# Per-token steps of a state-space block moved into the patch embedding's chunk pipeline

## The reference

```python
u = up_x @ W_up + b_up                      # up_x: the normed tokens
left, right = jnp.split(u, 2, axis=-1)      # 128 features each
conv = sum(conv_w[:, k] * xp[:, k:k + Lq, :] for k in range(3)) + conv_b
x = silu(conv)
delta = softplus(x @ W_delta + b_delta)
Bm = x @ W_B + b_B ; Cm = x @ W_C + b_C
# then over 37 positions: h = exp(delta*A)*h + (delta*x)*Bm ; y_t = h . Cm
gated = (y + D_skip * x) * silu(right)
```

## Time and profile before

| what | value |
|---|---|
| device time, median of 3 runs | 1154.97 us (1151.09 to 1156.85) |
| device time of the profiled execution | 1155.57 us |
| its span in the trace | 1153.4 us |
| busy: PE, DVE, ACT, POOL | 935.1, 657.2, 508.3, 305.0 us |
| DMA | 96.06 MB, 92705 packets |
| TensorE's granted clock over the run, in tenths, 40 slices | `9999656898898998998989999999979999998579999` |

### The profile page before, as it was taken

How to read it: one execution, slowest core, us unless ns; L and a number is a source line. 1 busy time by engine, 2 the same in 40 slices (tenths; PEclk the granted TensorE clock), 3 DMA queues, 4 the chain that set the end, 5 groups by cost and what they waited for, 6 DMA issues and landing times.

```text
span 1153.4 us, 17650 instructions
## 1 busy us (share of the span) xinstructions
PE 935.1 (81%) x5925; PEld 597.4 (52%) x5926; DVE 657.2 (57%) x1129; ACT 508.3 (44%) x1028; POOL 305.0 (26%) x361
## 2 busy tenths in 40 slices
PE   8996272677777777669999999989999997559996
PEld 6763230233333233235677777757767664336564
DVE  2534833588888889865454444437777673313332
ACT  1227371777777887424322222234444532223332
POOL 5913911133333430000000000035444430422222
PEclk9999656898898998989999999979999998579999
DMA  6292369422222211434521111000000000522230
GB/s 234 92 344 94 96 198 237 95 51 51 50 52 50 53 32 34 175 149 199 180 70 58 42 42 42 0 1 1 1 1 0 0 2 1 222 100 83 78 94 25
DMA packets 92705, 96.06 MB, mean 83 GB/s; under 512 B 64350, under 2 KB 78687, under 8 KB 90976
## 3 DMA queue, kind: packets, MB, share of 16 engines
q1 hardware_dynamic: 89904, 87.91, 25.1%
q0 software_dynamic: 2736, 7.30, 1.7%
HBM read 61.57 MB, written 34.59 MB: 83 GB/s over the span
## 4 chain that ended last, share of the span: by engine, by line
PE 64%; ACT 12%; DVE 9%; issue 6%; SPq 4%; DMA 4%; another core or an unknown queue 0%; POOL 0%; ACTq 0%; DVEq 0%; POOLq 0%
PE ps L526 8%; PE ps L585 8%; PE ps L1142 6%; ACT mem L1572 5%; PE ps L1024 4%; PE ps L1428 4%; PE ps L1444 4%; PE ps L1339 3%; PE ps L1273 3%; PE ps L395 3%; PE ps L1102 3%; PE ps L403 3%; SPq L783 2%; ACT mem L1597 2%; PE ps L1285 2%
## 5 line engine op out<-in xcount | busy, mean ns | idle before, releaser
L981 POOL TENSOR_TENSOR mem<-mem,sm 128x296 f32<-128x296 f32 x128 | 87.0, 713 | 364.3 <-ACT mem L1662 321.5
L1572 ACT ACTIVATE mem<-ps 128x512 f32<-128x512 f32 x288 | 154.0, 637 | 42.9 <-DMA factor_rows<-mem 30.3
L959 POOL TENSOR_SCALAR mem<-mem,sm 128x16 f32<-128x16 f32 x148 | 102.7, 716 | 203.5 <-PE ps L1142 203.5
L1102 PE MATMUL ps<-mem 64*128 64x128 bf16 x1140 | 92.0, 230 | 53.6 <-ACT mem L1572 44.3
L1102 PEld LDWEIGHTS ps<-mem 64*128 64x128 bf16 x1140 | 56.0, 99 | 121.6 <-ACT mem L1572 102.4
L1883 DVE TENSOR_TENSOR ps<-mem 128x512 f32<-128x512 f32 x144 | 93.5, 694 | 42.1 <-ACT mem L1597 41.6
L526 PE MATMUL ps<-mem 128*128 (+1 forms) x384 | 108.6, 413 | 0.6 <-DVE mem L499 0.6
L1597 ACT ACTIVATE mem<-ps 128x512 f32<-128x512 f32 x148 | 82.4, 609 | 54.0 <-PE ps L1109 53.8
L1142 PE MATMUL ps<-mem 128*32 128x512 f32 x592 | 87.3, 663 | 22.1 <-issue 13.6
L1109 PE MATMUL ps<-mem 64*128 64x512 bf16 x296 | 76.7, 421 | 31.5 <-DVE ps L1883 21.6
L1875 DVE TENSOR_TENSOR mem<-mem 128x1024 f32<-128x1024 f32 x72 | 87.7, 1218 | 25.0 <-ACT mem L1572 25.0
(11 more groups left out here) (224 smaller groups left out, 1613.0 us busy)
## 6 DMA issues: line engine op xcount, KB each, us to landing
mem<-gates SPq DMA_DIRECT2D x7, 1184.0 KB, 6.1
mem<-in_w SPq DMA_DIRECT2D x2, 4096.0 KB, 17.5
slots<-mem SPq DMA_DIRECT2D x1, 6682.0 KB, 23.8
mem<-slots SPq DMA_DIRECT2D x26, 257.0 KB, 2.7
mem<-in_patches SPq DMA_DIRECT2D x7, 864.0 KB, 4.8
mem<-factor_rows SPq DMA_DIRECT2D x296, 16.0 KB, 1.8
mem<-factor_rows SPq DMA_DIRECT2D x37, 128.0 KB, 2.3
mem<-delta_rows SPq DMA_DIRECT2D x9, 512.0 KB, 4.5
```

The costliest lines, as they stand in the source:

```text
L959: nc.gpsimd.tensor_scalar(c_win4[:, t % SLOTS * 2 + r, :, w0:w0 + 8].rearrange("p j (x i) -> p j x i", i=2)[:, :, :, i], c_all[:, r * 16:r ...
L1102: mm = nc.tensor.matmul(ps[:, ring_bank(at_), e * BT:(e + 1) * BT], a_stat[64 * r:64 * r + 64, g, e, :], delta_in[b % 2][64 * r:64 * r + 6 ...
L1572: nc.scalar.activation(decay_slots[b % 2][:, :, 4 * k:4 * k + 4], ps[:, ring_bank(at_), :].rearrange("p (e t) -> p t e", e=4), ACT.Exp).th ...
```

## The change

The step functions get five more stages. The hardware loop is replaced by 15 written-out steps, `chunks_in_step` with `LAG = 7`. In step k: the SiLU argument of chunk k-2; SiLU of chunk k-3 as exp(min(a,0) - log(1 + exp(-|a|))) for x and gate together (592 columns: two exponentials and a logarithm on ACT, two instructions on DVE); the products with that and C and delta's argument for chunk k-4; softplus and dx for chunk k-5; delta's pieces for chunks k-6 and k-7. No table load is left but the first. The products use the banks of the mean (4) and of the variance (5), so mean and variance wait for their evictions.

```diff
+LAG = 7
+def chunks_in_step(step):
+    for k in range(NCH + LAG):
+        step(k, k % 2, lambda d: 0 <= k - d < NCH)
...
             pe.wait_ge(embedded, k * 2 + 4)
+            if on(5):
+                pe.wait_ge(z_copied, k - 4)
             pe_mean(pe, ln, k - 1, 4)
         if on(0):
             products(1).then_inc(embedded_ps, 1)
+        if on(4):
+            c = k - 4
+            i = pair_rows(c)[0]
+            pe.wait_ge(x_ready, c + 1)
+            pe.wait_ge(LN["logvar"], LN_FROM[ln] + min(k - 2, NCH - 1) + 3)
+            if c >= 1:
+                pe.wait_ge(c_copied, c)
+            nc.tensor.matmul(ps[64 * i:64 * i + 64, 5, 0:CH], w_c, paired(xs, c * IC, IC),
+                             start=True, stop=True)
+            pe.wait_ge(LN["centered"], LN_FROM[ln] + min(k - 1, NCH - 1) + 3)
+            if c >= 1:
+                pe.wait_ge(z_copied, c)
+            nc.tensor.matmul(ps[:, 4, 0:CH], W("w_delta"), paired(xs, c * IC, IC),
+                             start=True, stop=True).then_inc(zc_ps, 1)
...
             mm.then_inc(up_ps, 1)
         if on(1):
+            if on(4):
+                pe.wait_ge(c_copied, k - 3)
             pe_var(pe, ln, k - 1, 1 - j, 5)
-    staged(pe, pe_embed, 2)
+    w_b, w_c = W("w_bc")[:, 0:N], W("w_bc")[:, N:2 * N]
+    chunks_in_step(pe_embed)
...
     def act_embed(k, j, on):
+        if on(3):
+            c = k - 3
+            now = sig[:, :, c % 2, :]
+            act.wait_ge(sig_cut, 2 * c + 1)
+            nc.scalar.activation(now, now, ACT.Exp).then_inc(sig_step, 1)
+            act.wait_ge(sig_step, 3 * c + 1)
+            nc.scalar.activation(now, now, ACT.Ln, bias=1.0).then_inc(sig_step, 1)
         if on(1):
             act_square(act, ln, k - 1, 1 - j)
...
+        if on(5):
+            c = k - 5
+            cs = ds(c * CH, CH)
+            act.wait_ge(soft_abs, c + 1)
+            nc.scalar.activation(delta[:, cs], delta[:, cs], ACT.Exp).then_inc(soft_step, 1)
+            act.wait_ge(soft_step, 2 * c + 1)
+            nc.scalar.activation(delta[:, cs], delta[:, cs], ACT.Ln, bias=1.0).then_inc(soft_step, 1)
+        if on(7):
+            c = k - 7
+            i, qs = pair_rows(c)
+            act.wait_ge(piece_cut, 2 * c + 1)
+            nc.scalar.activation(delta_part[:, 1, i, :, qs], cut_now, ACT.Copy).then_inc(piece_copied, 1)
+        if on(6):
+            c = k - 6
+            i, qs = pair_rows(c)
+            act.wait_ge(delta_ready, c + 1)
+            nc.scalar.activation(delta_part[:, 0, i, :, qs],
+                                 delta[:, c * CH:(c + 1) * CH].rearrange("p (q l) -> p l q", q=IC),
+                                 ACT.Copy).then_inc(piece_copied, 1)
+        if on(4):
+            c = k - 4
+            i, qs = pair_rows(c)
+            half = slice(64 * i, 64 * i + 64)
+            act.wait_ge(zc_ps, c + 1)
+            nc.scalar.activation(c_all[half, qs, :], ps[half, 5, 0:CH].rearrange("p (q l) -> p q l", q=IC),
+                                 ACT.Identity, bias=S("b_cc")[half]).then_inc(c_copied, 1)
+            if c >= 2:
+                act.wait_ge(delta_ready, c - 1)
+            nc.scalar.activation(z_now[:, c % 2, :], ps[:, 4, 0:CH], ACT.Identity,
+                                 bias=S("b_delta")).then_inc(z_copied, 1)
         if on(1):
             act_rstd(act, ln, k - 1, 1 - j, 5)
...
+        if on(3):
+            c = k - 3
+            cs = slice(c * CH, (c + 1) * CH)
+            now = sig[:, :, c % 2, :]
+            act.wait_ge(sig_cut, 2 * c + 2)
+            nc.scalar.activation(now, now, ACT.Exp).then_inc(sig_step, 1)
+    chunks_in_step(act_embed)
...
     def dve_embed(k, j, on):
+        if on(4):
+            c = k - 4
+            dve.wait_ge(sig_step, 3 * c + 3)
+            nc.vector.tensor_tensor(paired(xs, c * IC, IC), cv[:, c * IC:(c + 1) * IC, :],
+                                    sig[:, 0, c % 2, :].rearrange("p (i l) -> p i l", i=IC),
+                                    ALU.mult).then_inc(x_ready, 1)
+            nc.vector.tensor_tensor(sright[:, c * CH:(c + 1) * CH], sright[:, c * CH:(c + 1) * CH],
+                                    sig[:, 1, c % 2, :], ALU.mult).then_inc(right_ready, 1)
         if on(1):
             dve_center(dve, ln, k - 1, 4)
         if on(0):
...
                 nc.vector.tensor_tensor(hT0[:, m, ds(k * IC, IC), 1:L],
                                         ps[:, 2 * j + m, 0:IC * NP].rearrange("p (i l) -> p i l", i=IC),
                                         bc(posb[:, m, 1:L], 1, IC), ALU.add).then_inc(embedded, 1)
+        if on(5):
+            c = k - 5
+            cs = slice(c * CH, (c + 1) * CH)
+            dve.wait_ge(soft_step, 2 * c + 2)
+            nc.vector.scalar_tensor_tensor(out=delta[:, cs], in0=z_now[:, c % 2, :], scalar=0.0,
+                                           in1=delta[:, cs], op0=ALU.max,
+                                           op1=ALU.add).then_inc(delta_ready, 1)
         if on(1):
             dve_scale(dve, ln, k - 1, 1 - j)
+        if on(5):
+            dve.wait_ge(delta_ready, c + 1)
+            nc.vector.tensor_tensor(paired(dx, c * IC, IC), delta[:, cs].rearrange("p (q l) -> p q l", q=IC),
+                                    paired(xs, c * IC, IC), ALU.mult).then_inc(dx_ready, 1)
+        if on(3):
+            c = k - 3
+            now = sig[:, :, c % 2, :]
+            dve.wait_ge(sig_step, 3 * c + 2)
+            nc.vector.scalar_tensor_tensor(out=now, in0=both[:, :, c * CH:(c + 1) * CH], scalar=0.0,
+                                           in1=now, op0=ALU.min, op1=ALU.subtract).then_inc(sig_cut, 1)
         if on(2):
             c = k - 2
             images = ds(c * IC, IC)
...
                 nc.vector.scalar_tensor_tensor(out=cv[:, images, :], in0=leftp[:, images, s_:L + s_],
                                                scalar=w[:, s_:s_ + 1], in1=cv[:, images, :],
                                                op0=ALU.mult, op1=ALU.add).then_inc(conv_step, 1)
-    staged(dve, dve_embed, 2)
-    for q in range(NQ):
-        qs = slice(q * QT, (q + 1) * QT)
-        dve.wait_ge(z_copied, (q + 1) * NCH // NQ + 2)
-        nc.vector.scalar_tensor_tensor(out=delta[:, qs], in0=dz[:, qs], scalar=-1.0,
-                                       in1=dz[:, qs], op0=ALU.mult,
-                                       op1=ALU.min).then_inc(soft_abs, 1)
+            dve.wait_ge(conv_step, c * 3 + 3)
+            dve.wait_ge(up_right, c + 2)
+            if c >= 2:
+                dve.wait_ge(x_ready, c - 1)
+                dve.wait_ge(right_ready, c - 1)
+            arg = both[:, :, c * CH:(c + 1) * CH]
+            nc.vector.scalar_tensor_tensor(out=sig[:, :, c % 2, :], in0=arg, scalar=-1.0, in1=arg,
+                                           op0=ALU.mult, op1=ALU.min).then_inc(sig_cut, 1)
+        if on(7):
+            c = k - 7
+            i, qs = pair_rows(c)
+            dve.wait_ge(piece_copied, 2 * c + 2)
+            nc.vector.tensor_tensor(delta_part[:, 2, i, :, qs], cut_now, delta_part[:, 1, i, :, qs],
+                                    ALU.subtract).then_inc(piece_cut, 1)
+        if on(6):
+            c = k - 6
+            i, qs = pair_rows(c)
+            dve.wait_ge(piece_copied, 2 * c + 1)
+            if c >= 1:
+                dve.wait_ge(piece_cut, 2 * c)
+            nc.vector.tensor_tensor(cut_now, delta[:, c * CH:(c + 1) * CH].rearrange("p (q l) -> p l q", q=IC),
+                                    delta_part[:, 0, i, :, qs], ALU.subtract).then_inc(piece_cut, 1)
+        if on(4):
+            c = k - 4
+            cs = slice(c * CH, (c + 1) * CH)
+            dve.wait_ge(z_copied, c + 1)
+            nc.vector.scalar_tensor_tensor(out=delta[:, cs], in0=z_now[:, c % 2, :], scalar=-1.0,
+                                           in1=z_now[:, c % 2, :], op0=ALU.mult,
+                                           op1=ALU.min).then_inc(soft_abs, 1)
+    chunks_in_step(dve_embed)
```

```diff
-sp.wait_ge(empty_set, 2)
-sp.dma_start(slots.rearrange("(t p) w -> p t w", p=P), bc(empty, 1, ST)).then_inc(empty_out, 16)
...
+sp.wait_ge(piece_cut, CUTS)
+store_delta(0)
 sp.wait_ge(b_split, 4)
 store_b(0)
-sp.wait_ge(piece_cut, 3)
-store_delta(0)
 sp.wait_ge(zeros_set, 4)
 sp.wait_ge(delta_out, 16 * 6)
 load_delta(0)
-sp.wait_ge(piece_cut, 8)
+sp.wait_ge(piece_cut, CUTS + 2)
 store_dx(0)
 load_delta(1)
 sp.wait_ge(factors_out, 16 * 12)
 for t in range(INJ):
     load_inject(t)
-sp.wait_ge(piece_cut, 6)
 store_delta(1)
+sp.wait_ge(piece_cut, CUTS + DX_CUTS)
+store_dx(1)
 sp.wait_ge(b_split, 8)
 store_b(1)
-sp.wait_ge(piece_cut, 16)
-store_dx(1)
...
-sp.wait_ge(empty_out, 16)
 sp.wait_ge(scan_h, NCH + 2)
 sp.dma_start(w1s, w1).then_inc(ffn1_in, 16)
 sp.dma_start(w2s, w2).then_inc(ffn1_in, 16)
+sp.wait_ge(empty_set, 2)
+sp.dma_start(slots.rearrange("(t p) w -> p t w", p=P), bc(empty, 1, ST)).then_inc(empty_out, 16)
 sp_gates(sp, MOE["moe0"])
```

(15 more changed lines are left out.)

177 lines of the change are left out of this document (66 added, 111 removed).

## The result

Measured beside each other on one chip: before 1155.91 us (median of 4 runs, 1151.09 to 1158.05), changed 1189.11 us (4 runs, 1186.03 to 1191.06). The ratio is **1.029, with a 95% interval of 1.026 to 1.032**: slower. The forecast was 1182 us, slower. The profiled executions differ by 35.6 us in span (1189.0 against 1153.4).

What follows compares the result with a forecast made beforehand. Predicted bounds: TensorE up to 79 us, SyncE's queue of stores from 181 to 208.6. Later scan +15.0 and slot fill +12.4 on the profiled 1155.57 give 1183.0; the runs' median, 0.6 lower, 1182 us; range 1156 to 1196.

Steps and rivals of the forecast that it cites:

- mechanism A: Whole kernel: the closed loop of waits in the pipeline steps and the moved slot fill both cost; 1182 us, chance 0.52.
- The loop: Pipeline steps from 4 on: written orders close a chain through TensorE, ACT and DVE, 15.5 us per full step, 95.7 summed.
- Rival C: Steps 4 to 10: the seven-step lag hides the loop, TensorE's work sets 10.8 us per step; 1152 us, chance 0.18.
- E: Time at which DVE has finished the last delta piece: 141.6 us before, 149 predicted, bounds 144 and 163.
- the lower clock: TensorE, idling some 6 us per step from step 8, falls to 1.2 GHz: 4 us from step 9, bounds 0 and 8.
- the later start: Step 4's first product of C: predicted at 48.3 us, from 47.57 plus 0.7 for one new DVE instruction.
- GpSimd beside DVE: DVE slowed while POOL works on A's pieces until 61.0 us: 1.0 us taken, bounds nothing and 11.
- rival D: Step 4, until 61 us: GpSimd holds DVE's two-input instructions, costing 11 us instead of 1.0; 1193 us, chance 0.11.
- Behind E: SyncE's queue after the last delta piece: 28.9 us of splits, stores and loads before range 1's stores begin.
- the 45.7 of range 1: From the start of range 1's stores until the scan goes on: 45.7 us of transfers, whatever happened before.
- The fill: Slot fill moved ahead of the router's weights: delays them 10.3 us, plus 2.1 at TensorE's lower clock, +12.4 in all.
- The sum: +15.0 for the scan going on later and +12.4 for the fill: +27.4 on the profiled 1155.57 us.

Runs made afterwards that it cites:

- experiment 3: Changed kernel with another order inside a step: ScalarE's two copies and variance instructions earlier, VectorE's softplus maximum behind the scaling; 1179.77 us, ratio 1.022.
- experiment 4: Changed kernel with products of no use put into TensorE's waits behind the up product and the variance, steps 7 to 10; 1188.77 us, ratio 1.030.
- experiment 7: Changed kernel with the edits of experiment 1 and experiment 3 together; 1165.87 us, ratio 1.010.
- experiment 8: Changed kernel with the edits of experiment 7 and experiment 4, and range 1's stores laced between the first three injections' loads; 1167.69 us, ratio 1.013.
- experiment 9: Experiment 7's kernel with half of delta's stores and the gate's first half issued early, and B's range-0 bias ahead of DVE's last piece; 1162.39 us, ratio 1.008.
- experiment 1: Changed kernel with the fill of the slots issued behind the gates' transfers instead of ahead of them; 1176.96 us, ratio 1.019.
- experiment 11: Experiment 9's kernel with the first three injections' 27 loads issued by GpSimd; 1151.17 us, ratio 0.998.
- experiment 10: Kernel before with the first three injections' 27 loads issued by GpSimd instead of SyncE; 1146.7 us, ratio 0.992.
- experiment 2: Kernel before with only the fill of the slots moved to the change's place, with the empty row it copies; 1168.91 us, ratio 1.012.
- experiment 5: Kernel before with range 1's stores of delta and dx issued ahead of the first three injections' 27 loads; 1154.85 us, ratio 1.000.
- experiment 6: Kernel before with range 1's stores of delta, B and dx laced between the first three injections' loads; 1153.89 us, ratio 1.000.

## Why the prediction was right, and where its sizes were off

The sign, the forecast's mechanism A and the range held. Step by step:

- **The loop.** Predicted 12.2, 13.4, 14.6, 15.5, 15.5, 11.1, 4.3, 9.1; measured 13.1, 13.7, 14.2, 15.4, 19.0, 13.0, 4.7, 10.1. Rival C (a step of 10.8, TensorE's work) is out, and experiment 3 shows that the chain is one of order: changing it alone took 6.8 us off. TensorE's work in a step, put at 10.8, was 11.4 to 11.5.
- **E: 149 predicted, 152.9 measured.** The mis-sized term is the lower clock, 4 by the prediction. In step 8 the products on the path take, at 0.59 of the clock, 0.83 (C and delta's), 1.78 (up: 3.93 against 2.15) and 0.82 (variance) more than in step 7 (from start to start): 3.4 of the 3.6 between the two steps. In step 9 the first two are 0.8 each, of 1.9; the last two terms are 1.4 over, and with the clock kept up in experiment 4 they were 4.2 and 9.0, which is 1.6 less than here. Together 6.4 where 4 was allowed, under the upper bound of 8. Experiment 4 got 4.4 of it back. The other 1.5 of the 3.9 is the later start (49.6 for 48.3) and steps 4 and 5 (1.2 too long in sum), less the 1.0 allowed for GpSimd.
- **GpSimd beside DVE.** The prediction looked at this from 48 us on, and the larger part came before. While GpSimd ran its tensor_tensors (33.1 to 37.6), the two L1855 took 4.62 (1.09 alone) and the negation L1864, a new instruction, 1.57 (0.77 alone); TensorE then waited 1.78 us ahead of the variance, where it waited 0.53 in the kernel before (at 39.66), for the centring and the square behind them:

```profile
33.25 4.62 DVE L1855 SCALAR_TENSOR_TENSOR mem<-mem,sm 128x296 f32<-128x296 f32 x2
...
41.57 1.26 PE L407 MATMUL ps<-mem,ones 128*128 128x296 f32 x4 [1.78 <-ACT mem L414]
```

  These 1.3 us are the later start, by their size. Whether they are paid depends on under a microsecond of timing: in experiments 7, 8 and 9 the two L1855 had got through first (1.09), L1864 took 2.6, TensorE did not wait, and step 4 began at 47.2, 47.2 and 46.8; in experiments 1, 3, 4 and 11 the two took 4.6, TensorE waited 2.1 to 2.3, and step 4 began at 50.3 to 50.6. So up to 3 us of E go with it from one execution to the next, most of them this wait. From 43 us on, beside tensor_scalars of about 2.9 us each, four places were longer than alone: L437 1.22 for 0.77, L1851 0.66 and 1.23 for 0.43, the two L1855 1.82 for 1.09, 2.2 in sum, of which 0.8 inside step 4. None of these was held for a whole GpSimd instruction, and step 4 lasted 13.1, so rival D falls with its 11 us, though its mechanism is there at the size of 1 to 2. All of this was read from rows; no run moved GpSimd's work away.
- **Behind E.** 28.9 predicted to range 1's stores, 30.8 measured (dx's stores held the queue for 5.0 and not 4.0, the 27 loads for 13.5 and not 12.75); the 45.7 of range 1 became 46.9. With E that makes 21.9 instead of 15.0. Experiments 9 and 10 qualify the step "whatever happened before": with half of delta's stores taken out the 45.7 became 41.4, and with the loads going beside them 49.6.
- **The fill.** 10.3 + 2.1 predicted, 12.2 + 1.8 in the trace, and 12.2 and 14.4 us in the time by experiments 1 and 2. The weights' loads (issued at 555.4, 19.6 us to landing) were out of the way at 575, as predicted (554.1 and the shift of 21.9 give 576.0); the fill (issued at 556.2, 42.8 to landing) ended at 599.0, so it took some 24 us and not 18.5. The rate was mis-sized: 315 and 338 GB/s in the two stretches shown above, where the rate of before was 371. Another part of the sum went the other way: the 16 KB landed at 597.4, 1.6 us ahead of the fill's end, where the prediction had them 1.5 behind it.
- **The sum.** +27.4 predicted; +35.6 between the profiled executions, +33.2 between the medians.

The gates' row bears out the Trainium skill (DMA: Bandwidth & Descriptors, section "Queues, rings and completion order"), which has each engine take one ring's descriptors in order: 13.3 us for 16 KB behind the fill. In experiment 10 the loads stand in another queue of the profile's list (q0, the stores in q1) and were no longer held by them for their issue, only slower to land (7.0 us for 16 KB, 1.9 before). The same section says that an engine with work in several queue rows takes turns between them, which agrees.

What stays open: why the clock fell for 5 us in experiment 4, what the loop would cost with GpSimd's work out of its way, and how much of the change's loss was from the new instructions themselves and not from their order; no run took them out.

## What to carry to other kernels

Work that is spread over a pipeline's steps is free only if no engine's instruction order makes one step wait for another engine's late part of the same step: lay the written orders of all engines side by side and add up the closed chain, not each engine's busy time. A large transfer that nobody waits for belongs behind, not ahead of, the small ones that somebody does. Where a wait ends on stores and the same queue also issues loads, a reordering may give nothing; a second engine's queue gave 9 us. And where two engines get in each other's way, as GpSimd and DVE do here from 33 to 39 us, one profile shows one alignment: look at several before calling the cost small.

## What the runs showed of the hardware that was not expected

- The DMA engines were filled to 1.05 in a stretch that had stood at 0.26, and the time did not change (experiments 5 and 6): their busy share told nothing of what the queue's order would give.
- GpSimd issued 27 loads in 14.7 us (0.51 us for each of 16 KB, 0.79 for one of 128 KB), SyncE in 12.75. The stores beside them took 15.3 us to land, where they took 12.6 before.
- Two DVE instructions of 0.55 us each took 4.62 in sum beside GpSimd's tensor_tensors, and 1.09 in executions in which they came a microsecond earlier.
- TensorE's granted clock fell to 0.64 for 4.8 us in which it was busy all the time (experiment 4).
- Products put into the waits raised the clock of a stretch from 0.59 to 0.91, but the up product of step 8 still ran slow (3.10 for 2.15), in a step that began behind 3.0 us of idle time.
